# A four-layer network on one core: TensorE multiplies constants in front of its long waits

## The reference

```python
x = x + L0_attn(layernorm(x), Wq, Wk, Wv, Wo)              # 16 heads of 32, 4 KV heads
x = x + L0_ffn(layernorm(x), ternary gate, up, down)       # silu(g)*u, scaled rows
x = x + L1_attn(layernorm(x), gamma, beta, W.., b..)       # 16 heads of 32, with biases
x = x + L1_ffn(layernorm(x), router, ...)                  # mixture of depths: top 64 of 512 rows
x = x + L2_attn(layernorm(x), q_w, kv_w, o_w)              # 4 heads of 128, rotary
x = x + L2_ffn(layernorm(x), w_fc, w_proj)                 # ternary weights, gelu, quantised rows
x = x + L3_attn(layernorm(x), wq_comp, wq_up, wk, wv, ..)  # 16 heads of 128, out_w1, out_w2
x = x + L3_ffn(layernorm(x), lut, gate_idx, up_idx, ..)    # weights = lut[idx], silu(g)*u
```

## Time and profile before

| what | value |
|---|---|
| median of three runs | 3383.57 us |
| the three runs | 3386.67, 3377.07, 3383.57 us |
| profiled execution, span | 3376.4 us (its own device time is not given beside it; 7.2 under the median) |
| instructions | 46857 |
| PE busy | 2992.2 us (89%), 16388 matmuls |
| DVE busy | 1996.1 us (59%) |
| ACT busy | 1551.2 us (46%) |
| POOL busy | 1019.2 us (30%) |
| DMA | 105.51 MB, mean 31 GB/s |

### The profile page before, as it was taken

The page is one execution under the profiler, slowest core; times in us unless marked ns, Lnnn a source line. Parts: engine busy times, 40 slices in busy tenths (PEclk is TensorE's granted clock), DMA queues, the critical chain, the costliest instruction groups (busy, mean ns, idle before and its releaser), DMA issues. The chain is left out here.

```text
span 3376.4 us, 46857 instructions
## 1 busy us (share of the span) xinstructions
PE 2992.2 (89%) x16388; PEld 2260.9 (67%) x16388; DVE 1996.1 (59%) x5348; ACT 1551.2 (46%) x3598; POOL 1019.2 (30%) x1143
## 2 busy tenths in 40 slices
PE   6999799997999977978788767998689999989999
PEld 4777678885666645446566646775467777768887
DVE  5666587775555554233747767664678777742121
ACT  5777566664666652133222244444455555531000
POOL 3655333222444530000156640000133233322222
PEclk9999899998999987988899988999799999999999
DMA  2000301101000021203100020003100000020000
GB/s 87 2 2 1 113 32 32 32 32 63 1 2 1 2 67 64 100 7 117 66 4 4 2 101 1 1 1 119 34 1 1 1 1 1 1 103 13 13 13 13
DMA packets 65872, 105.51 MB, mean 31 GB/s; under 512 B 9315, under 2 KB 29795, under 8 KB 65509
## 3 DMA queue, kind: packets, MB, share of 16 engines
q1 hardware_dynamic: 65222, 102.41, 8.7%
q0 software_dynamic: 416, 0.10, 0.0%
HBM read 89.75 MB, written 12.85 MB: 30 GB/s over the span
## 5 line engine op out<-in xcount | busy, mean ns | idle before, releaser
L714 POOL TENSOR_SCALAR a_P<-a_P,a_rec 128x512 f32<-128x512 f32 (+3 forms) x256 | 301.5, 1190 | 350.9 <-DVE a_rec L872 350.9
L402 ACT ACTIVATE tree_value<-tree_bit,table_lut,tree_step 128x256 f32<-128x256 uint8 x496 | 275.3, 595 | 140.8 <-DVE tree_value L416 73.0
L416 DVE COPY_PREDICATED tree_value<-tree_bit,tree_value 128x256 f32<-128x256 uint8 x434 | 235.0, 547 | 133.3 <-ACT tree_value L402 104.9
L787 ACT ACTIVATE a_P<-a_P,a_low 128x384 f32<-128x384 f32 (+3 forms) x512 | 281.7, 558 | 25.0 <-DVE a_low L866 24.9
L101 PE MATMUL bank<-f_xT_hi,f_w_hi 128*128 128x512 f32 (+1 forms) x704 | 276.6, 393 | 14.0 <-DVE f_w_lo L1214 14.0
L102 PE MATMUL bank<-f_xT_hi,f_w_lo 128*128 128x512 f32 (+1 forms) x704 | 276.1, 392 | 0.0
L103 PE MATMUL bank<-f_xT_lo,f_w_hi 128*128 128x512 f32 (+1 forms) x704 | 275.7, 392 | 0.0
L1136 POOL CAST f_h_hi<-f_sg 128x512 fp32r<-128x512 f32 (+1 forms) x88 | 84.5, 961 | 587.6 <-DVE f_sg L1236 297.8
L866 DVE CUSTOM_DVE_ANT_0 a_P<-bank,a_causal 128x384 f32<-128x384 f32 (+3 forms) x512 | 222.9, 482 | 63.1 <-PE bank L949 62.6
L794 ACT ACTIVATE a_PT<-bank 128x512 f32<-128x512 f32 x320 | 174.2, 594 | 83.3 <-PE bank L960 82.6
L1236 DVE TENSOR_TENSOR f_sg<-bank,f_sg 128x512 f32<-128x512 f32 (+1 forms) x44 | 30.4, 691 | 269.4 <-PE bank L103 269.4
(11 more groups left out here) (464 smaller groups left out, 7922.7 us busy)
## 6 DMA issues: line engine op xcount, KB each, us to landing
f_w_raw<-in_f_w SPq DMA_DIRECT2D x11, 768.0 KB, 12.8
f_w_raw<-table_w SPq DMA_DIRECT2D x11, 768.0 KB, 11.2
tree_idx<-in_f_idx SPq DMA_DIRECT2D x62, 128.0 KB, 2.1
table_w<-tree_value SPq DMA_DIRECT2D x62, 128.0 KB, 1.7
x_res<-in_x SPq DMA_DIRECT2D x4, 1024.0 KB, 10.8
m_piece<-in_m_wq SPq DMA_DIRECT2D x2, 2048.0 KB, 12.1
m_piece<-in_m_wo SPq DMA_DIRECT2D x2, 2048.0 KB, 8.5
m_piece<-in_m_w_gate SPq DMA_DIRECT2D x2, 2048.0 KB, 10.4
```

Source lines behind the costliest of these rows:

```text
L402: act.activation(prog.tree_value[(h + to) % 4][:, :], prog.tree_bit[h % 2][0][:, :], ACT.Identity, bias=prog.table_lut[:, 2 * k:2 * k + 1] ...
L416: dve.copy_predicated(prog.tree_value[(h + keep) % 4][:, :], prog.tree_bit[h % 2][bit][:, :], prog.tree_value[(h + other) % 4][:, :]).then ...
L714: last = pool.tensor_scalar(Pr[j][:, g, col:col + n], Pr[j][:, g, col:col + n], rec[:, j, i, g:g + 1], None, ALU.mult)
L787: last = act.activation(Pr[j][:, k, col:col + n], Pr[j][:, k, col:col + n], ACT.Exp, bias=low[:, j, i, k:k + 1], scale=-1.0, accum_out=tot ...
```

## The change

A helper `spin` issues n matmuls on PE. Each multiplies the bf16 identity with the bf16 masks and writes 128x256 into the first 256 columns of a bank. Nothing reads the result: the next job of the same bank overwrites it. The helper is called at sixteen places (thirteen calls in the code, of which three serve two places each), with n from 22 to 115, 898 products in all. At each place the wait for the bank's vacancy now stands in front of the products, and the wait for the data behind them; nothing else is changed.

| stage | ahead of | products |
|---|---|---|
| f0 | first gate | 40 |
| a1 | first T; first Q | 45; 75 |
| m1, routing | row; pos; selT | 95; 32; 62 |
| m1, chosen rows | hT; hT2 | 33; 33 |
| f2 | turn; total_of; inner; turn_hidden 0 and 1 | 105; 33; 33; 36 and 22 |
| a3, weights | first W | 75 |
| a3, main | first T | 115 |
| f3 | first gate | 64 |

```diff
+def spin(pe, prog, out, n):
+
+    for _ in range(n):
+        pe.matmul(out, prog.ident_b[:, :], prog.mask_b[:, :, :].rearrange("p a n -> p (a n)"), start=True, stop=True, skip_group_check=True)
...
                 if kind == "T":
                     for tt in range(TT):
+                        if tt == 0:
+                            pe.wait_ge(*vacant(key))
+                        if at == 0 and k == 0 and tt == 0 and biased:
+                            spin(pe, prog, ps[J.bank(key)][:, 0:2 * P], 45)
                         if k == 0:
                             pe.wait_ge(*c_xn(0, at * TT + tt + 1))
-                        if tt == 0:
-                            pe.wait_ge(*vacant(key))
...
                     pe.wait_ge(*c_xlo(0, at * DC + DC))
                     pe.wait_ge(*vacant(key))
+                    if at == 0 and k == 0 and kind == "Q" and biased:
+                        spin(pe, prog, ps[J.bank(key)][:, 0:2 * P], 75)
                     if at == 0 and k == 0:
                         pe.wait_ge(*c_wlo(0, {"Q": 1, "K": 2, "V": 3, "VT": 3}[kind]))
...
                 if j == 0:
                     for tt in range(TT):
                         pe.wait_ge(*read("T", b, tt))
+                if b == 0 and j == 0:
+                    pe.wait_ge(*vacant("G", 0, 0))
+                    spin(pe, prog, ps[J.bank(("G", 0, 0))][:, 0:2 * P], 40 if scaled else 64)
...
             def turn(t):
+                pe.wait_ge(*vacant("T", t))
+                if t == 0:
+                    spin(pe, prog, ps[5][:, 0:2 * P], 105)
                 pe.wait_ge(*c_xn(0, t + 1))
-                pe.wait_ge(*vacant("T", t))
...
             def turn_hidden(t):
+                pe.wait_ge(*vacant("H", t, 0))
+                if t < 2:
+                    spin(pe, prog, ps[H_BANK[0]][:, 0:2 * P], (36, 22)[t])
                 pe.wait_ge(*h_ready(0, t + 1))
...
         def _(pe):
+            pe.wait_ge(*JW.vacant(("W", 0, 0), 0))
+            spin(pe, prog, ps[JW.bank(("W", 0, 0))][:, 0:2 * P], 75)
             for g in range(4):
                 pe.wait_ge(*w_in[g](0, 32))
...
                     tt = job[2]
+                    pe.wait_ge(*vacant(*job))
+                    if n == 0 and tt == 0:
+                        spin(pe, prog, bank(*job)[:, 0:2 * P], 115)
                     pe.wait_ge(*c_xn(0, n * TT + tt + 1))
-                    pe.wait_ge(*vacant(*job))
...
                 if kind == "row":
+                    pe.wait_ge(*vacant("row", b))
+                    if b == 0:
+                        spin(pe, prog, ps[0][:, 0:2 * P], 95)
                     pe.wait_ge(*c_diag(0, (b + 1) * TT))
-                    pe.wait_ge(*vacant("row", b))
```

More of the change, by code:

```diff
@@ L1978, in total_of @@
             def total_of(g, c):
+                pe.wait_ge(*vacant("sum", g))
+                if g == 0:
+                    spin(pe, prog, ps[7][:, 0:2 * P], 33)
                 pe.wait_ge(*c(0, 4))
-                pe.wait_ge(*vacant("sum", g))
                 pe.matmul(ps[7][:, 0:4], prog.ones[:, :], sums[:, 4 * g:4 * g + 4], start=True, stop=True).then_inc(J.fills(("sum", g)), 1)
@@ L1985, in inner @@
                 for n in range(4):
+                    pe.wait_ge(*vacant("F", t, n))
                     if t == 0:
+                        if n == 0:
+                            spin(pe, prog, ps[n][:, 0:2 * P], 33)
                         pe.wait_ge(*c_tern(0, n + 1))
-                    pe.wait_ge(*vacant("F", t, n))
                     for k in range(DC):
@@ L2849, in _ @@
                 elif kind == "pos":
+                    pe.wait_ge(*vacant("pos", b))
+                    if b == 0:
+                        spin(pe, prog, ps[3][:, 0:2 * P], 32)
                     pe.wait_ge(*c_kept(0, b + 1))
-                    pe.wait_ge(*vacant("pos", b))
                     for tt in range(TT):
@@ L2858, in _ @@
                     s = b // 2
+                    pe.wait_ge(*vacant("selT", b))
+                    if b == 0:
+                        spin(pe, prog, ps[2][:, 0:2 * P], 62)
                     pe.wait_ge(*c_sel(0, b + 1))
-                    pe.wait_ge(*vacant("selT", b))
                     for tt in range(TT):
@@ L3119, in transposed_rows @@
                 for s in range(ST):
+                    pe.wait_ge(*J.vacant((what, s), 0))
+                    if s == 0:
+                        spin(pe, prog, ps[s][:, 0:2 * P], 33)
                     pe.wait_ge(*c_h(0, done + s + 1))
-                    pe.wait_ge(*J.vacant((what, s), 0))
                     for k in range(DC):
```

## The result

| | before | changed |
|---|---|---|
| median | 3381.69 us (4 runs, 3377.07 to 3386.67) | 3395.94 us (4 runs, 3392.68 to 3397.69) |
| profiled execution, span | 3376.4 us | 3395.4 us |

The changed kernel takes 14.3 us longer. The ratio is 1.0044, with a 95% interval from 1.003 to 1.0058, that is 10 to 20 us. The forecast was 8.9 us longer, in a range of 3380 to 3403.

What follows compares the result with a forecast made beforehand. PE, busy 89%, was taken to bound the kernel; terms -12.7 - 5.7 - 2.5 + 0.3 + 9.5 - 0.4 + 2.6 sum to 8.9 us slower, 3383.6 + 8.9 = 3392.5 us, range 3380 to 3403.

Steps and rivals of the forecast that it cites:

- the products start at about 2403.0, not at 2388: Window attention's T: 115 products wait for the block's barrier, so T moves back 15.2 us; net -12.7.
- Rival A: Waits are open from their start, PE enters the new block alone, nothing is late: 3364 us; chance 0.10.
- rival D: Products do not raise the clock at all, T moves back 24.5 us: over 3450 us; chance 0.04.
- Q: Attention32 (a1): 75 products behind the xT_lo wait take 10.0 us, Q starts at 808.9; with T net -5.7.
- f3: Lookup feed-forward: 64 products behind the reads of the T banks, 7.7 us warm; taken -2.5 (-2.0 to -3.7).
- I take 2.5: Window attention's T: us given back where PE ran at half clock, at most 3.4.
- the mixture of depths, +9.5: Five places in m1 together win 9.5 us, bounds +4 to +10.5.
- The gather at 1284.45 ran 6.35 us at half clock, all of it on the path: m1 routing: full clock in the gather wins 3.2 us, since DVE is idle there.
- 4.0 us each, room about 4: m1's second block: two places of 33 products fit and win 3.1 and 2.4 us.
- f0, f2 and a3's weights: Scaled feed-forward +0.3, ternary feed-forward -0.4, window attention's weights +2.6 us.
- a weak sign: From 786.2 identity multiplications kept PE busy 4.36 of 4.4 us at 0.50; taken as transposes not raising the clock, unlike products.
- Rival C: Short places (row, turn, weights) are late and the m1 chain wins only 4: 3404 us; chance 0.17.

Runs made afterwards that it cites:

- experiment 3: Kernel before plus only 125 products at the end of a3's weights block, ahead of the barrier: 1.2 us faster (4.7 faster to 1.4 slower).
- experiment 1: Changed kernel without a1 T, a1 Q, a3 T and f3 products: 6.0 us faster than before; those four alone: 22.5 us slower.
- experiment 5: Products only at long waits the change leaves alone: 3.4 us faster than before; together with the four late places moved to idle time: 10.9 us faster.
- experiment 6: Late places moved plus further waits, without f2's 72 and 22 products: 17.8 us faster than before; also without all f2 and hT products: 13.8 us faster.

## Why the prediction was right, and where not

**Right: the listed wait is not the room.** The step on which the sum rested, "the products start at about 2403.0, not at 2388", came out: the products and DVE's a_xn both begin at 2406.45 in the changed kernel. T moved back 14.6 us (15.2 behind its block's start where it was 0.6); the forecast was 15.2. That it is so near owes something to two errors of opposite sign: the start at half clock took 5.5 us, taken 4.5 (a mean clock of 0.82 over 15.3 us), and a product at full clock 0.109 us, taken 0.12. Rival A needed the products before the barrier, and rival D a clock of 0.50 under them; their window shows 0.82. Both fell.

**Right in mechanism, small in size: Q.** The wait for xT_lo ended the idle time as forecast, and the products took 10.8 us, taken 10.0. Q began 24.4 us into its block where 23.3 (808.9 less 785.64) was said. The stage grew 8.7 for a forecast of 5.7; 1.2 of the 3 us is this (24.43 less 23.26), the rest is within what a0 varies by.

**Right: f3.** 64 products at full clock from 4.7 us behind the block's first instruction (3013.02) took 6.9 us; the forecast was 7.7. The first gate product came 3.45 us later in its block than before, and 4.1 us that ran at half clock now ran at full, which gives back 2.05: net 1.4, and the stage table has +1.5 for a forecast of +2.5.

**Wrong: what is given back at a3 T.** "I take 2.5" for full clock in the transposes and the first products. The chain from the first transpose to the first product of L101 takes 6.0 us where it took 7.4 (the earlier trace rows has its end at 2411.03), but then the products run at half clock for 4.6 us (2427.7 to 2432.3), where they did for 2.8. The clock was at 1.00 under the first eight transposes and through the idle 2.1 us behind them, and fell under the second eight, some 3.9 us after the stream of products had ended; it stayed down through the next 1.6 us of idle time and the products behind:

```profile
2425.30:2425.80 0.50, 0.50 (x6) 0.39 (x4) 0.00 (x0) 0.30 (x1) 0.00 (x0) 0.82 0.00 0
2425.80:2426.10 0.30, 0.28 (x2) 0.00 (x0) 0.00 (x0) 0.29 (x1) 0.00 (x0) 0.50 0.00 0
```

The give-back was some 0.5 instead of 2.5, and +14.1 is 14.6 less that. I had asked whether the clock is up when the products end, and not whether it is still up where it is used.

**Wrong: the mixture of depths, +9.5.** Measured by itself it is 1.9 (7.4 at most). Two steps failed. The first is "The gather at 1284.45 ran 6.35 us at half clock, all of it on the path", for 3.2 us. In the changed kernel the clock is 1.00 when the gather begins (1287.98) and drops a microsecond later, and the stretch took 9.0 us at 0.62, where the same instructions had taken 8.9 (1284.45 to the next position products at 1293.33). The only idle time between the 62 products and the drop are the 2.4 us ahead of the gather. In six other traces with the 62 products the first gather ran at full clock for half of its time or throughout, but in four of these the second, at 1.00 before, was then partly at 0.50: the step looked at one of four gathers. The position products ahead of it did win: the gather began 1.3 us earlier in its block, for 0.8 forecast. The second step is "4.0 us each, room about 4" for hT. The room was 1.3 us, because PE's first instruction of the block waits for the biases until 2.2 us into it. That term had taken its room from the length of a wait (4.5), the very reading that it corrected at T. hT2, the other place of 33, had its room: its transposes stand 2.0 us later in the block than before, the first products behind the gate product 0.5 earlier, so that about the 2.4 us of the forecast were won there. The prediction had named both faults as the bound of +4 ("if the clock falls again behind the 62 and the two 33 are a little late"); it gave them too little weight.

**Not to be told apart: f0, f2 and a3's weights.** f0 and f2 were forecast to win next to nothing, and -1.9 and -0.2 in the stage table are within what a0 varies by. At a3's weights the clock is 1.00 at the a_w products, and the stage is 1.2 us shorter for a forecast of 2.6, within that variation too.

**The price of a product** was taken as 0.12 from fp32r products; at full clock it is 0.109 (the 125 of experiment 3 took 13.81 us, of which the last by itself is 0.27). The Trainium skill, "TensorE: Matmul & The Clock Gate", section "Back-to-back issue gap", gives N/2.4 + 2.5 ns for a matmul by itself, 109 ns at N = 256; these runs agree, with a weight load for each product. The difference makes 1 us at the largest place.

**Two small slips and a weak sign.** 64 products from a cold start end at 3009.6 by the prediction's own rule and not at 3009.3, and in rival D the 75 ahead of the weights overrun by 5.8 us and not by 7 to 9; neither changes a bound that mattered. And that 4.4 us of transposes stayed at 0.50 does not tell transposes from products: the first 5.5 us of T's 45 products in a1 were at 0.50 as well (a mean of 0.64 over 7.6 us).

**The sum** was 8.9 for 14.3. The losses were put at 20.9 and measured 22.5 (experiment 1), the gains were put at 12.0 and measured 6.0. The size was off on the side of the gains. Rival C lowered them for a partly wrong reason: the short margins of row, turn and weights held (PE still waited 1.2, 1.0 and 0.9 us behind the products there), and hT's did not.

## What to carry to other kernels

A long wait in a table tells how long an engine had nothing to do, not from when a new instruction in front of it could run: look for what stands between the two, a barrier, or a second data wait such as the one for the biases at hT. Products that are to raise the clock must be able to run while PE is idle, on the near side of a barrier or ahead of the second wait, and they won where dense work followed at once (attention512); at a3's T, with two idle stretches of about 2 us in the work behind them, they cost their own time behind the barrier and won nothing ahead of it. 898 products of which a third came late cost 14 us, while 1431 (17819 matmuls less 16388), put where PE is idle, won 17.8. Whether the clock is up must be read where it is used, and over more than one execution.

## What the runs showed of the hardware

- The granted clock can fall when PE is already at work again. It was 1.00 when the gather began 2.4 us after a stream of 7 us, and fell within a microsecond of work, to stay at 0.50 for 6.8 us although PE was busy all the time (9.02 of 9.02 us in the window). Behind T's products in the changed kernel it fell under the second eight transposes. I had expected continuous work to be safe from it.
- The same program text does not give the same clock each time. After 125 products the transposes ran at 1.00 behind idle times of 1.8 and 2.6 us (experiments 3 and 5) and at 0.50 behind one of 2.1 (experiment 6). A stretch of m1's second block was at 0.50 for 23.9 us on end in one trace and for 37.5 in another (experiment 5). What decides is not shown.
- Products that multiply constants raise the clock: 45 of them went from 0.50 to 1.00 within 7.6 us at a1 (mean 0.64). Once the clock was up, fp32 transposes kept their half length: 1.04 us for eight behind T's products, where they had taken 1.97.
